# Unread matmuls placed differently around the first attention maxima of a two-layer transformer kernel

## The chip, the cores and the metric

The kernel runs on one core of one Trainium2 chip. The metric is device time in microseconds (us), the median of the runs of a kernel.

## The reference

Input x is 8 batches of 512 tokens of 128 values. Four blocks follow one another, each as x = layernorm(x + block(x)); the change touches the PE order around the first of them, causal attention with 16 heads of size 8:

```python
k, q, v = (einsum('bte,fe->btf', x, W).reshape(B, T, 16, 8) for W in (Wk, Wq, Wv))
k, q = _layernorm(k, kln_g, kln_b), _layernorm(q, qln_g, qln_b)
dot = einsum('bihd,bjhd->bhij', q * E ** -0.25, k * E ** -0.25)
att = softmax(where(causal, -inf, dot), axis=-1)
out = einsum('bte,fe->btf', einsum('bhij,bjhd->bihd', att, v).reshape(B, T, E), Wo) + bo
```

The other three are a soft mixture of 8 experts with 64 slots each, a delta-rule attention (a sequential scan) with a gated feed-forward layer, and a feed-forward layer with ternary weights.

## The kernel before

Each engine has a program of its own in which the order of its instructions is written out by hand; semaphores tie the programs together. PE, the matmul engine, runs a preparation for batch 0 and then a sequence of slots. In a slot (`slot(b, moe, front, tail, before)`) up to four batches are at work at once: `b` is in its attention scores, exponentials and products, `moe` in the experts, `tail` in the projections of the next attention, and `front` in its query, key and value projections and the first part of its row maxima. Only the first slot has a `front` and a `b` and neither of the others: `slot(0, None, 1, None, first[0])`. After the slots the second half of the kernel follows (the scan and the two feed-forward layers), from about 830 us on.

**Maxima.** The softmax needs the maximum of each row of scores. It is found with scores of its own: a batch has 24 units (`x_units`, `scores_for_maxima`). A unit is two or four matmuls of q and k on L954 (32 rows of the array each, 128 to 512 columns), two small bf16 matmuls that add the causal mask on L957, and then one DVE reduction out of PSUM on L1797. Of a batch, units x0 to x18 (`X_LATE` = 19) are run ahead, for batch 0 in the preparation and for the others at the end of a slot; the last five (e19 to e23) stand at the start of the batch's own slot, between its first scores. Units x0, x1, x12, x13 have four matmuls of 128 columns, x2, x3, x14, x15 four of 256, x4 to x7 and x16 to x18 two of 384, x8 to x11 two of 512. A unit has two PSUM banks of four, so that unit k waits until DVE has reduced unit k-2.

**Unread matmuls.** `idle_matmuls(n, bank=6)` (L964) issues n bf16 matmuls of 128x512 whose result nobody reads; they keep PE at work. In the preparation 64 of them stand between the last transposes and the maxima of batch 0, and two ahead of each unit. At the end of a slot two stand ahead of each of the units x14 to x18 (`if x_at > NM_AT`), and none ahead of x0 to x13.

**Ahead of the first unit** q and k, split in high and low parts, go to DRAM and back to be spread over the partitions. SyncE's queue writes them with six transfers (`q_rep<-hilo`, `k_rep<-hilo`, L541), each adding 16 to `split_stored`; it waits for all of them (`CREDIT + 96`) and then loads `qr` and `kr` (L546), for which unit x0 waits on PE (`rep_loaded`).

**End of the first slot.** PE runs the products of the last head group (L991), turns them (`turn_products`, L923), turns the attention (`transpose_att`, L923) and projects it (`project_att`, L1009); ACT or DVE must evacuate each before the next. Then `maxima_to` runs the units of batch 1. DVE adds the residual and works out the layer norm of batch 0 between its reductions.

Of the kernel before, what the change touches and what calls it, by code (L numbers as in the profile page):

```python
# [41 lines left out]
NM_AT, XR_AT = 13, 14  # L42
# [7 lines left out]
CREDIT = 1  # L50
# [93 lines left out]
def build(nc, A, out, taps=None):  # L144
    ctx = ExitStack()
    with ctx:
# [3 lines left out]
        def sem(name):  # L150
            return ctx.enter_context(nc.semaphore(name))
# [80 lines left out]
        class Heads:  # L232

            def __init__(self, c):
# [107 lines left out]
                  for k in range(2)]  # L342
# [35 lines left out]
        split_done, split_stored, rep_loaded = sem("split_done"), sem("split_stored"), sem("rep_loaded")  # L378
# [65 lines left out]
                  + [(A2, "n0", 4), (A2, "n1", 5), (A2, "n2", 0), (A2, "n3", 1), (A1, "fo", 3),  # L444
                     (A2, "y", 5), (A1, "x3T", 4)])
        ring2 = Ring(None, [(hand, use) for hand, use, _ in turns2], {use: bank for _, use, bank in turns2})


# [256 lines left out]
        def _(g):  # L705
# [132 lines left out]
            def out_products(t, h, half, r):  # L838

                cs = slice(half * HALF, (half + 1) * HALF)  # L840
                if r == 0:
                    g.wait_ge(hist_kept, CREDIT + t * 4 + 2 * half + 2)
                    g.wait_ge(om_summed, CREDIT + t * 8)
                    if half == 1:
                        g.wait_ge(ln3_done, CREDIT + t * DVE_LN)
                qc = s_qc[h].rearrange("p (c j) d -> p c j d", j=CH)
                _, at = PAIRS[r]
                g.tensor_tensor(o_m[half][r][:, :, :, 0:HD], state[h][:, cs, :, :],  # L848
                                qc[:, cs, r, :].unsqueeze(2).broadcast_to([P, HALF, HD, HD]), ALU.mult)
                g.tensor_tensor(o_m[half][r][:, :, :, HD:HD + r + 1], u_c[h][:, cs, :, 0:r + 1],  # L850
                                s_qkd[h][:, cs, at:at + r + 1].unsqueeze(2).broadcast_to([P, HALF, HD, r + 1]), ALU.mult) \
                    .then_inc(om_made, 1)
# [44 lines left out]
        def _(pe):  # L897
# [18 lines left out]
            def fill(use, turn):  # L916
                ring.wait_free(pe, use, *turn)
                return ps[:, ring.bank(use), :]

            def transposes(use, turn, srcs):  # L920
                bank = fill(use, turn)
                for k, src in enumerate(srcs):
                    last = pe.transpose(bank[0:src.shape[1], k * P:(k + 1) * P], src, ident[:, :])  # L923
                return last
# [15 lines left out]
            def scores_for_maxima(b, use, turn):  # L940

                k = int(use[1:])
                if k == 0:
                    pe.wait_ge(rep_loaded, CREDIT + (b + 1) * 32)
                it, pr, gs = x_units[k]
                pairs.wait_free(pe, use, *turn)
                at = pairs.bank(use)
                w = (it + 1) * P
                banks = [ps[:, at + n, 0:len(gs) * w].rearrange("p (n w) -> p n w", w=w) for n in range(2)]
                for j, gg in enumerate(gs):  # L950
                    for n, bank in enumerate(banks):
                        q = 2 * pr + n
                        rows = slice(32 * q, 32 * q + 32)
                        pe.matmul(bank[:, j, :], qr[rows, gg, it * P:(it + 1) * P], kr[rows, gg, 0:w],  # L954
                                  start=(j == 0), stop=False)
                for bank in banks:
                    last = pe.matmul(bank[:, :, it * P:w], ident_b[:, :],  # L957
                                     mask_qk[:, :].unsqueeze(1).broadcast_to([P, len(gs), P]), start=False, stop=True)
                last.then_inc(s_ready, 1)

            def idle_matmuls(n, bank=6):

                for _ in range(n):
                    pe.matmul(ps[:, bank, :], ident_b[:, :], mask_qk[:, :].unsqueeze(1).broadcast_to([P, 4, P]),  # L964
                              start=True, stop=True)

            def transpose_maxima(b, turn, h):
                pe.wait_ge(s_taken, CREDIT + b * NX + (h + 1) * (NX // 2))
                transposes(f"nm{h}", turn, [neg_max[:, 8 * h:8 * h + 8, :].rearrange("p h t -> p (h t)")]) \
                    .then_inc((f_ready, k_ready)[h], 1)  # L970
# [26 lines left out]
            def turn_products(b, turn, gg):  # L997
                pe.wait_ge(pv_act, CREDIT + V.emptied(f"pvT{gg}", b))
                transposes(f"pv{gg}", turn, [pv_T[:, gg % 2, t * P:(t + 1) * P] for t in range(NT)]).then_inc(n_ready, 1)
# [5 lines left out]
            def project_att(b, turn):  # L1005
                pe.wait_ge(n_act, CREDIT + N1.emptied("aT", b))
                bank = fill("ao", turn)
                for t in range(NT):
                    last = pe.matmul(bank[:, t * P:(t + 1) * P], act_T[:, t * P:(t + 1) * P], w_out[:, :],  # L1009
                                     start=True, stop=True)  # L1010
                last.then_inc(n_ready, 1)
# [36 lines left out]
            def expert_hidden(b, turn, c):  # L1048
                pe.wait_ge(t_act, CREDIT + T.emptied("slots", b))
                pe.matmul(fill(f"h{c}", turn), e_w1[:, c * P:(c + 1) * P], slots, start=True, stop=True) \  # L1050
                    .then_inc(t_ready, 1)
# [21 lines left out]
            def transpose_x2(b, turn):  # L1073
                pe.wait_ge(x2_ready, CREDIT + b + 1)
                transposes("x2T", turn, [y_sq[:, t, :] for t in range(NT)]).then_inc(g_ready, 1)
# [7 lines left out]
            def slot(b, moe, front, tail, before):  # L1083
# [83 lines left out]
                            products(b, gg - 1, jt)  # L1167
                if moe is not None:
                    expert_hidden(moe, turn, 0)
                if b is not None:  # L1170
                    turn_products(b, turn, 3)
                if moe is not None:
                    expert_hidden(moe, turn, 1)
                if b is not None:
# [4 lines left out]
                if tail is not None:  # L1179
                    if moe is None:  # L1180
                        idle_matmuls(40)
                    transpose_x2(tail, turn)
                if b is not None:
                    project_att(b, turn)
                x_at = 0

                def maxima_to(end):
                    nonlocal x_at
                    while x_at < end:
                        if front is not None:  # L1190
                            if x_at > NM_AT:
                                idle_matmuls(2)
                            scores_for_maxima(front, f"x{x_at}", turn)
                        x_at += 1

                maxima_to(2)
                for j in range(4):
                    if tail is not None:
                        project(tail, turn, j)
                    maxima_to(3 + j)  # L1200
                for half in range(2):
                    if moe is not None:
                        expert_out(moe, turn, (2 * half, 2 * half + 1))
                    maxima_to(8 + 2 * half)
# [26 lines left out]
            transpose_qk(0, first, 0)  # L1231
            transpose_qk(0, first, 1)
            pe.wait_ge(slot_taken, 1)
            idle_matmuls(64)
            for k in range(X_LATE):
                idle_matmuls(2)
                scores_for_maxima(0, f"x{k}", first)
                if k == NM_AT:
                    transpose_maxima(0, first, 0)
            now = slot(0, None, 1, None, first[0])  # L1240
            pe.wait_ge(w_final, 2)
            now = slot(1, 0, 2, None, now)
            now = slot(2, 1, 3, 0, now)
            with pe.Fori(0, B - 4) as i:
                slot(i + 3, i + 2, i + 4, i + 1, {N1: i + 2, K: i + 2, XE: i + 2, AS: i + 2, T: i + 1, F: i + 3, XL: i + 3, G: i})
# [952 lines left out]
```

## Time and profile before

| | us |
|---|---|
| median of 3 runs | 1388.12 |
| lowest, highest | 1379.6, 1394.48 |
| profiled execution, device time | 1389.59 |
| its span, first to last instruction | 1387.9 |
| PE busy | 1187.7 (86%) |
| DVE busy | 928.8 (67%) |
| ACT busy | 624.3 (45%) |

Times in the profile count from the first instruction. The granted clock (PEclk) is the share of PE's full clock, 2.4 GHz, that the chip let it have in a stretch: it is 1.00 or 0.50 (1.2 GHz), and a number between them is the mean of a stretch that holds both. Over the whole span it is 0.916.

### The profile page before, as it was taken

The numbers are of one execution on the slowest core, as the hardware profiler recorded it, in microseconds if no ns is written. First come the engines' busy times: TensorE is split into PE (matmuls) and PEld (weight loads), VectorE is DVE, ScalarE is ACT, GpSimd is POOL, SyncE is SP. The second block draws the span as 40 slices with busy tenths as digits, with TensorE's granted clock in tenths as the row PEclk, the third lists the DMA queues.
The fourth block names the chain that finished last, engine by engine and source line by source line (L and its number), as shares of the span: only waits on it lengthen the run. The fifth ranks groups of instructions, "written<-read, shape, count | busy, mean of one in ns | idle before, by whom it ended". The sixth has DMA issues, their size and how long they took to land.

```text
span 1387.9 us, 19758 instructions
## 1 busy us (share of the span) xinstructions
PE 1187.7 (86%) x6115; PEld 622.6 (45%) x6115; DVE 928.8 (67%) x2401; ACT 624.3 (45%) x1194; POOL 454.1 (33%) x466
## 2 busy tenths in 40 slices
PE   5898989899999899999988571158999999999997
PEld 3333445355453554535545340124455455455453
DVE  3343636556668677686865767888888888889321
ACT  1043372753736637466365320203455544645642
POOL 3022130221314333143323045125545534544510
PEclk8677899999999999999989895578999999999999
DMA  4103021032131423304212148320120220200000
GB/s 107 71 2 106 9 81 36 1 107 64 47 93 32 139 63 78 92 32 139 55 34 48 41 102 203 91 48 12 44 64 9 56 56 16 56 23 8 24 8 8
DMA packets 85755, 79.90 MB, mean 58 GB/s; under 512 B 42800, under 2 KB 63408, under 8 KB 83632
## 3 DMA queue, kind: packets, MB, share of 16 engines
q1 hardware_dynamic: 85680, 79.01, 21.0%
q8 instruction: 33, 0.54, 0.2%
q14 instruction: 42, 0.34, 0.1%
HBM read 43.17 MB, written 35.00 MB: 56 GB/s over the span
## 4 chain that ended last, share of the span: by engine, by line
PE 54%; DVE 21%; ACT 10%; issue 9%; POOL 4%; DMA 1%; SPq 1%; DVEq 0%; ACTq 0%; POOLq 0%
PE ps L1294 10%; PE ps L1277 6%; PE ps L954 5%; PE ps L923 4%; PE ps L991 4%; DVE arena L1797 4%; ACT arena L1431 3%; ACT arena L1393 3%; PE ps L957 3%; PE ps L964 3%; PE ps L980 3%; PE ps L1285 2%; PE ps L1050 2%; PE ps L1058 2%; PE ps L1040 2%
## 5 line engine op out<-in xcount | busy, mean ns | idle before, releaser
L1797 DVE TENSOR_REDUCE arena<-ps 128x4 f32<-128x512 f32 (+2 forms) x192 | 198.5, 1043 | 99.9 <-PE ps L957 96.9
L1294 PE MATMUL ps<-arena,late 128*128 128x512 f32 x512 | 224.5, 592 | 0.0
L1393 ACT ACTIVATE arena<-ps 128x512 f32<-128x512 f32 (+2 forms) x200 | 109.6, 566 | 242.8 <-PE ps L923 123.2
L753 POOL TENSOR_SCALAR_AFFINE_SELECT arena<-arena 128x512 f32<-128x512 f32 x128 | 83.5, 655 | 319.7 <-ACT arena L1431 318.4
L1431 ACT ACTIVATE arena<-ps 128x1024 f32<-128x1024 f32 (+3 forms) x256 | 169.8, 710 | 37.2 <-PE ps L980 35.8
L964 PE MATMUL ps<-mask_qk,ident_b 128*128 128x512 bf16 x447 | 129.8, 410 | 31.9 <-DVE arena L2076 31.9
L1294 PEld LDWEIGHTS ps<-arena,late 128*128 128x128 f32 x512 | 96.2, 190 | 115.8 <-issue 114.3
L1580 ACT ACTIVATE arena<-ps,f_s 128x512 f32<-128x512 f32 x128 | 85.6, 688 | 105.6 <-PE ps L1294 95.5
L1277 PE MATMUL ps<-arena,late 128*128 128x512 f32 x256 | 118.5, 617 | 7.8 <-ACT arena L1580 7.3
L923 PE MATMUL ps<-ident,arena 128*128 128x128 f32 (+1 forms) x624 | 103.8, 301 | 23.1 <-ACT arena L1393 13.5
L848 POOL TENSOR_TENSOR arena<-arena 128x512 f32<-128x512 f32 x64 | 81.5, 1273 | 119.8 <-DVE slot_T L2093 75.4
L1393 ACT ACTIVATE arena<-ps,arena 128x128 f32<-128x128 f32 (+1 forms) x128 | 62.4, 529 | 126.2 <-DVE arena L1824 52.1
L954 PE MATMUL ps<-kr,qr 32*128 32x512 f32 (+3 forms) x512 | 99.4, 427 | 15.3 <-ACT arena L1431 6.1
L991 PE MATMUL ps<-arena 128*32 128x512 f32 (+3 forms) x1024 | 99.5, 474 | 10.2 <-ACT arena L1393 10.2
L923 PEld LDWEIGHTS ps<-ident,arena 128*128 128x128 f32 (+1 forms) x624 | 74.0, 150 | 64.4 <-ACT arena L1393 23.3
L980 PE MATMUL ps<-qr,kr 32*128 32x256 f32 (+3 forms) x512 | 82.2, 435 | 18.5 <-DVE arena L1797 7.8
L954 PEld LDWEIGHTS ps<-kr,qr 32*128 32x128 f32 x512 | 47.2, 202 | 99.2 <-issue 38.2
L980 PEld LDWEIGHTS ps<-qr,kr 32*128 32x128 f32 x512 | 37.6, 193 | 110.5 <-ACT arena L1431 59.1
L1277 PEld LDWEIGHTS ps<-arena,late 128*128 128x128 f32 x256 | 49.0, 196 | 69.7 <-issue 58.3
L964 PEld LDWEIGHTS ps<-mask_qk,ident_b 128*128 128x128 bf16 x447 | 45.2, 104 | 75.9 <-issue 46.3
L1833 DVE RECIPROCAL arena<-ps 128x16 f32<-128x16 f32 x32 | 8.2, 256 | 99.3 <-PE ps L923 98.9
L957 PE MATMUL ps<-mask_qk,ident_b 128*128 128x128 bf16 (+1 forms) x384 | 66.9, 260 | 0.0
(186 smaller groups left out, 1953.4 us busy)
## 6 DMA issues: line engine op xcount, KB each, us to landing
qr<-q_rep SPq DMA_DIRECT2D x8, 1024.0 KB, 5.7
kr<-k_rep SPq DMA_DIRECT2D x8, 1024.0 KB, 8.0
scan_d<-late SPq DMA_DIRECT2D x56, 138.0 KB, 3.0
arena<-scan_d SPq DMA_DIRECT2D x12, 552.0 KB, 6.9
q_rep<-hilo SPq DMA_DIRECT2D x24, 256.0 KB, 3.1
k_rep<-hilo SPq DMA_DIRECT2D x24, 256.0 KB, 3.9
proj_d<-arena SPq DMA_DIRECT2D x8, 768.0 KB, 5.1
late<-proj_d SPq DMA_DIRECT2D x8, 768.0 KB, 4.5
```

The costliest lines, as they stand in the source:

```text
L923: last = pe.transpose(bank[0:src.shape[1], k * P:(k + 1) * P], src, ident[:, :])
L954: pe.matmul(bank[:, j, :], qr[rows, gg, it * P:(it + 1) * P], kr[rows, gg, 0:w], start=(j == 0), stop=False)
L957: last = pe.matmul(bank[:, :, it * P:w], ident_b[:, :], mask_qk[:, :].unsqueeze(1).broadcast_to([P, len(gs), P]), start=False, stop=True)
L964: pe.matmul(ps[:, bank, :], ident_b[:, :], mask_qk[:, :].unsqueeze(1).broadcast_to([P, 4, P]), start=True, stop=True)
L980: last = pe.matmul(ps[:, pairs.bank(f"s{k}") + n, 0:S - jt * P], kr[rows, gg, jt * P:(jt + 1) * P], qr[rows, gg, jt * P:S], start=True, st ...
L991: last = pe.matmul(bank[32 * h4:32 * h4 + 32, jt * P:S], v_aug[:, jt, 4 * gg + h4, :], prob[:, gg % 2, h4, p_off[jt]:p_off[jt] + S - jt * ...
L1277: return pe.matmul(ps[:, ring2.bank(use), :], w, src, start=True, stop=True)
L1294: last = pe.matmul(ps[:, ring2.bank(f"{n}{c}"), :], w[:, k, c * P:(c + 1) * P], src[:, k, :], start=(k == 0), stop=(k == HC - 1))
L1393: return act.activation(dst, src(ps[:, bank, :]), func, **kw)
L1431: act.activation(prob[:, gg % 2, 2 * pr:2 * pr + 2, p_off[jt]:p_off[jt] + w], ps[:, bank:bank + 2, 0:w], ACT.Exp).then_inc(p_taken, 1)
L1580: return act.activation(dst, src(ps[:, ring2.bank(use), :]), func, **kw)
L1797: v.tensor_reduce(heads[:, 2 * pr:2 * pr + 2, gs[0]:gs[-1] + 1], ps[:, at:at + 2, 0:len(gs) * w].rearrange("p q (n w) -> p q n w", w=w), X ...
```

## The change

Ahead of the maxima of batch 0 the 64 unread matmuls become 44, then a wait for `split_stored`, then 36; ahead of each of the 19 units one stands in place of two. In the first slot (`chain_only`), four are added ahead of `turn_products(b, turn, 3)`, four ahead of `transpose_att`, four ahead of `project_att` and two behind it, and two ahead of each of the units x0 to x13. Those in the middle of the slot write bank 0, the others bank 6. Nothing changes on the other engines.

```diff
@@ slot @@
+                chain_only = b is not None and moe is None and tail is None
+                if chain_only:
+                    idle_matmuls(4, 0)
                 if b is not None:
                     turn_products(b, turn, 3)
+                if chain_only:
+                    idle_matmuls(4, 0)
...
                     transpose_x2(tail, turn)
+                if chain_only:
+                    idle_matmuls(4, 0)
                 if b is not None:
                     project_att(b, turn)
+                if chain_only:
+                    idle_matmuls(2, 0)
...
                         if front is not None:
-                            if x_at > NM_AT:
+                            if x_at > NM_AT or chain_only:
                                 idle_matmuls(2)
                             scores_for_maxima(front, f"x{x_at}", turn)
@@ preparation @@
             pe.wait_ge(slot_taken, 1)
-            idle_matmuls(64)
+            idle_matmuls(44)
+            pe.wait_ge(split_stored, CREDIT + 96)
+            idle_matmuls(36)
             for k in range(X_LATE):
-                idle_matmuls(2)
+                idle_matmuls(1)
                 scores_for_maxima(0, f"x{k}", first)
```

PE's rows around the first unit, with the semaphores that they wait for (the first of the two unread matmuls of x0 is counted with the fill). Before:

```order
L964 MATMUL ps<-mask_qk,ident_b 128x512 [waits slot_taken]
L964 MATMUL ps<-mask_qk,ident_b 128x512 x65
L954 MATMUL ps<-kr,qr 128x128 [waits rep_loaded]
L954 MATMUL ps<-kr,qr 128x128 x3
L957 MATMUL ps<-mask_qk,ident_b 128x256 x2
L964 MATMUL ps<-mask_qk,ident_b 128x512 x2
L954 MATMUL ps<-kr,qr 128x128 x4
```

PE's rows at the same place, changed:

```order
L964 MATMUL ps<-mask_qk,ident_b 128x512 [waits slot_taken]
L964 MATMUL ps<-mask_qk,ident_b 128x512 x43
L964 MATMUL ps<-mask_qk,ident_b 128x512 [waits split_stored]
L964 MATMUL ps<-mask_qk,ident_b 128x512 x36
L954 MATMUL ps<-kr,qr 128x128 [waits rep_loaded]
L954 MATMUL ps<-kr,qr 128x128 x3
L957 MATMUL ps<-mask_qk,ident_b 128x256 x2
L964 MATMUL ps<-mask_qk,ident_b 128x512
L954 MATMUL ps<-kr,qr 128x128 x4
```

The 66 in one piece became 44 and 37 with a wait between them, and two between the units became one.

PE's rows from the last products of the first slot (L991) over the transposes (L923) and the projection (L1009) to its first units of batch 1. Before:

```order
L991 MATMUL ps<-arena 32x128 x4
L923 MATMUL ps<-ident,arena 128x128 x8
L1009 MATMUL ps<-w_out,arena 128x128 x4
L954 MATMUL ps<-kr,qr 128x128 x4
L957 MATMUL ps<-mask_qk,ident_b 128x256 x2
L954 MATMUL ps<-kr,qr 128x128 x4
L957 MATMUL ps<-mask_qk,ident_b 128x256 x2
```

PE's rows at the same place, changed:

```order
L991 MATMUL ps<-arena 32x128 x4
L964 MATMUL ps<-mask_qk,ident_b 128x512 x4
L923 MATMUL ps<-ident,arena 128x128 x4
L964 MATMUL ps<-mask_qk,ident_b 128x512 x4
L923 MATMUL ps<-ident,arena 128x128 x4
L964 MATMUL ps<-mask_qk,ident_b 128x512 x4
L1009 MATMUL ps<-w_out,arena 128x128 x4
L964 MATMUL ps<-mask_qk,ident_b 128x512 x4
L954 MATMUL ps<-kr,qr 128x128 x4
L957 MATMUL ps<-mask_qk,ident_b 128x256 x2
L964 MATMUL ps<-mask_qk,ident_b 128x512 x2
L954 MATMUL ps<-kr,qr 128x128 x4
```

Sixteen unread matmuls came in between the products and unit x0, and two ahead of each of the 13 units that follow.

## Rows read from the trace of the kernel before

**Rows 1.** Stretches of the start: each engine's busy us (x instructions), granted clock, DMA.

```profile
26.10:39.30 13.20, 13.18 (x61) 5.78 (x59) 0.00 (x0) 0.00 (x0) 4.62 (x3) 1.00 0.54 177
44.30:73.80 29.50, 29.47 (x107) 11.76 (x107) 14.98 (x16) 0.00 (x0) 0.00 (x0) 0.50 0.00 1
73.80:77.50 3.70, 3.70 (x25) 1.71 (x26) 3.27 (x4) 0.00 (x0) 0.00 (x0) 0.99 0.02 4
77.50:90.90 13.40, 11.60 (x59) 5.07 (x57) 6.84 (x7) 7.80 (x17) 4.14 (x5) 1.00 0.00 0
90.90:108.00 17.10, 15.80 (x85) 5.58 (x85) 5.91 (x14) 11.92 (x17) 5.79 (x7) 0.50 0.01 2
87.50:90.90 3.40, 2.34 (x16) 1.14 (x15) 2.35 (x2) 1.23 (x3) 2.36 (x3) 1.00 0.00 0
128.50:131.80 3.30, 2.38 (x20) 1.34 (x21) 3.14 (x13) 0.00 (x0) 1.26 (x1) 1.00 0.00 0
131.80:152.30 20.50, 19.67 (x80) 8.96 (x81) 16.50 (x31) 0.69 (x2) 0.00 (x0) 0.50 0.05 14
```

**Rows 2.** PE in order of time, fill and first unit: start, length, instructions, [idle before].

```profile
23.70 15.57 PE L964 MATMUL ps<-mask_qk,ident_b 128*128 128x512 bf16 x66
44.33 0.69 PE L954 MATMUL ps<-kr,qr 32*128 32x128 f32 x4 [5.05 <-DMA kr<-k_rep]
```

**Rows 3.** SyncE's queue in order of time: the load that follows the wait for `split_stored`.

```profile
35.61 0.37 SPq L546 DMA_DIRECT2D qr<-q_rep  x1
```

**Rows 4.** PE in order of time, the unread pairs between units at 1.2 GHz.

```profile
45.35 1.06 PE L964 MATMUL ps<-mask_qk,ident_b 128*128 128x512 bf16 x2
...
47.36 1.06 PE L964 MATMUL ps<-mask_qk,ident_b 128*128 128x512 bf16 x2
...
49.48 1.06 PE L964 MATMUL ps<-mask_qk,ident_b 128*128 128x512 bf16 x2
...
56.98 1.06 PE L964 MATMUL ps<-mask_qk,ident_b 128*128 128x512 bf16 x2
...
58.77 1.06 PE L964 MATMUL ps<-mask_qk,ident_b 128*128 128x512 bf16 x2
...
60.67 1.06 PE L964 MATMUL ps<-mask_qk,ident_b 128*128 128x512 bf16 x2
```

**Rows 5.** The same at 2.4 GHz: units with two unread matmuls, then with one.

```profile
75.44 0.59 PE L964 MATMUL ps<-mask_qk,ident_b 128*128 128x512 bf16 x2
...
76.46 0.59 PE L964 MATMUL ps<-mask_qk,ident_b 128*128 128x512 bf16 x2
...
77.93 0.38 PE L964 MATMUL ps<-mask_qk,ident_b 128*128 128x512 bf16 x1
...
78.73 0.59 PE L964 MATMUL ps<-mask_qk,ident_b 128*128 128x512 bf16 x2
```

**Rows 6.** DVE in order of time: reductions of a unit of each size.

```profile
45.60 0.69 DVE L1797 TENSOR_REDUCE arena<-ps 128x4 f32<-128x512 f32 x1 [22.71 <-PE ps L957]
...
49.72 1.23 DVE L1797 TENSOR_REDUCE arena<-ps 128x4 f32<-128x1024 f32 x1 [1.43 <-PE ps L957]
...
53.63 0.96 DVE L1797 TENSOR_REDUCE arena<-ps 128x2 f32<-128x768 f32 x1 [0.57 <-PE ps L957]
```

**Rows 7.** PE in order of time, end of the first slot.

```profile
124.59 0.66 PE L923 MATMUL ps<-ident,arena 128*128 128x128 f32 x4 [0.78 <-ACT arena L1393]
125.99 0.66 PE L923 MATMUL ps<-ident,arena 128*128 128x128 f32 x4 [0.75 <-DVE arena L1838]
127.33 1.16 PE L1009 MATMUL ps<-w_out,arena 128*128 128x128 f32 x8 [0.69 <-ACT arena L1393]
128.57 0.44 PE L954 MATMUL ps<-kr,qr 32*128 32x128 f32 x4
...
144.53 1.06 PE L964 MATMUL ps<-mask_qk,ident_b 128*128 128x512 bf16 x2
...
155.65 1.88 PE L1020 MATMUL ps<-slot_T,arena 128*128 128x512 f32 x4
```

## The prediction

> **What bounds the kernel now.** I read the granted clock first, then the stretches of the first 155 us in which it changes, and then PE, DVE and SyncE's queue in order of time inside them. The change edits nothing behind the first slot, so only this start can gain or lose by itself; the other 1230 us can differ only by where the clock falls and rises.
>
> The start is a clock story. Unread matmuls run at 2.4 GHz until about 39.3 us; then PE stands for 5.05 us until the load of kr has landed [rows 2]. When it resumes at 44.33 the clock is at 1.2 GHz, and it stays there for 29.5 us in which PE is busy without a pause, with two unread matmuls in each unit [rows 1]. There PE sets the pace: DVE needs 0.69 us for a unit of 512 scores, 0.96 for 768, 1.23 for 1024, and waits before each [rows 6]; PE's units follow each other at 2.01 us (four matmuls of 128 columns), 2.12 (four of 256), 1.79 (two of 384) and 1.90 (two of 512), read as differences between the starts of successive unread pairs [rows 4]. At 73.8 the clock returns, and a unit of two of 384 with two unread matmuls takes 1.02 us, with one 0.80 [rows 5]. The clock holds for the first third of the first slot (to 90.9), is at 1.2 GHz again to 108, and again from 131.8 to 152.3, in which the 14 units of batch 1 that have no unread matmuls lie almost whole [rows 1, 7].
>
> **The two-part fill.** An unread matmul costs 0.216 us at 2.4 GHz: 61 records in 13.2 us [rows 1]. Taking 22 away lets the first part end about 4.75 us earlier than 39.27 (15.57 us from 23.70 [rows 2]), at 34.5. PE then waits for `split_stored`. SyncE issues the load of qr right behind the same wait, at 35.61 [rows 3]; so PE stands about 1 us. 36 and the one ahead of x0 take 37 x 0.216 = 8.0 us, to about 43.6. The kr load is not touched and lands at 44.33 as before, so x0 starts at 44.33 in either kernel: the fill costs and gains nothing in itself, and no gap is over 1.1 us. Nothing but PE's own units is queued behind the new wait. The clock outlasted most of a gap of 5.05 us in the trace [rows 2], so I expect it at 2.4 GHz when x0 starts.
>
> **One unread matmul a unit.** Here I had to choose. At 2.4 GHz a 384-column unit with one is 0.80 us of PE against 0.96 of DVE, and the 512-column units are further apart (1.23 of DVE). DVE then sets the pace and PE stands for a sixth to a third of the time, its work mostly the 32-row matmuls. Which stretch is that nearest to? From 73.8 to 77.5 the units had two each, PE was busy 3.70 of 3.70 us, and the clock held. From 87.5 to 90.9 units with one each stood among first scores and waits, 2.34 of 3.40 us busy, and the clock fell at their end; from 128.5 to 131.8 units with none, 2.38 of 3.30, and it fell [rows 1]. One unread matmul in a DVE-paced row is nearer to the two that fell. So I expect the clock to hold for the first units, on the strength of the fill just before them, and to fall after about as much of such work as went before the fall at 90.9 (3.4 us), near 47.7, give or take 2. Once it is at 1.2 GHz, 29.5 us with two unread matmuls a unit did not raise it [rows 1]; one will do so less.
>
> The price: at 1.2 GHz a unit gets shorter by one unread matmul, 0.43 us (512 columns), so 1.58, 1.69, 1.36 and 1.47 us, all above DVE's time. 4 x 1.58 + 4 x 1.69 + 7 x 1.36 + 4 x 1.47 = 28.5, and 0.2 for the small transpose between: 28.7 us. The first three units at 2.4 GHz save 0.6 to 0.7 each: 26.6 us. Before, 44.33 to 77.5 were 33.2 us. **Gain 6.5 us.** (With all at 1.2 GHz, 4.5.)
>
> **What is late next.** The first slot's opening third then begins at 1.2 GHz instead of 2.4. Before, it took 13.40 us with PE busy 11.60 [rows 1]. Work of this kind stretches by 1.79 / 1.02 = 1.75 [rows 4, 5]: 11.60 x 1.75 = 20.3 us, and the small waits for ACT and DVE vanish in it. **Loss 6.9 us**, if the clock does not rise among the projections (L932) of this stretch; it can, and then half comes back. From 90.9 on the stretch was at 1.2 GHz anyway (17.1 us, busy 15.8 [rows 1]); whether a stretch of full clock comes a little earlier or later there is worth a few us either way, and I put it at zero.
>
> **The filled end of the first slot.** The four unread matmuls ahead of each of three steps take 0.86 us where PE stood 0.78, 0.75 and 0.69 [rows 7]: 0.36 us more, all told. The two behind `project_att` and the two ahead of x0 lie under DVE, whose residual and statistics begin at the end of the projection too. Sixteen unread matmuls (3.5 us at 2.4 GHz) and the transposes and projection between them (0.66 + 0.66 + 1.16) are 6 us of work with hardly a pause, so the clock should be up when x0 starts, even if it wasn't. Units x0 to x13 took 128.57 to 144.53, 16 us, although PE ran at 1.2 GHz for most of it; DVE was nearly always busy (16.50 of the 20.5 us from 131.8, nearly all in its first part) [rows 1, 7]. With two unread matmuls at 2.4 GHz PE needs 1.02 for a unit where DVE needs 0.96 and its small steps, and less than DVE elsewhere: no cost. The gain is behind them: from 144.53 to 152.3, 7.8 us at 1.2 GHz with two unread matmuls a unit, become 7.8 / 1.75 = 4.4, if the clock holds through x13: 3.4 saved. **Gain 3.0 us** with the 0.36 taken off.
>
> **The sum** is -6.5 + 6.9 - 3.0 = -2.6 us: 1387.0 by the profiled execution (1389.6), 1385.5 by the median (1388.1). The profiled execution stands 1.5 us above the median, well inside the runs' spread of 15 us, so I take the median's: 1385.5 us.
>
> **Rivals.** *One is enough*: the clock holds through all 19 units. For it: the fill now runs up to the first unit, and there is no gap over about 0.5 us. Against it: the two stretches above. Then DVE paces: four units at about 0.9, eight at 1.23 less 0.06 overlap, seven at 0.96 less 0.06, and 0.5 to the first reduction: 3.6 + 9.4 + 6.3 + 0.5 = 19.8 us, 13.4 less than before; the first third of the slot keeps its clock. 1388.1 - 13.4 - 3.0 = 1371.7. The Trainium skill (TensorE: Matmul & The Clock Gate, Part 1, "What's actually happening") says that the throttled state is the default and "activity releases the throttle", and its table "Why this matters for your kernels" asks only that there be no long idle gaps between bursts. By it this rival would be the outcome. The trace disagrees in part: 29.47 of 29.50 us busy at a clock of 0.50 [rows 1].
>
> *Rise among the projections*: as forecast, but the clock comes back within the slot's first third. Half of 6.9: 1382.
>
> *Slower, the clock falls in the second row of units*: those of 512 columns last 1.23 us on DVE with 2 x 0.216 unread in them, a thinner mix than the 384-column units for which the trace shows a held clock. If it falls at x8, PE needs 1.90, 2.01 instead of 1.23 and 0.8 to 1.2 for six units: about 0.67 x 4 + 0.9 x 2 = 4.5 us lost, and the 3.4 behind them are not gained. Sum -6.5 + 6.9 + 0.4 + 4.5 = +5.3: 1393. It decides from the first unit at 1.2 GHz; if that were x0, all 14 would run as at 45 to 70 us, 27 us instead of 16, and the time would be 1400.
>
> *The fill doesn't do what it says*: if the clock were at 1.2 GHz when the second part starts, 37 x 0.43 = 15.8 us would end at 51.4, 7 us behind kr's landing. Then 28.7 us of units: +7.1 - 4.5 + 6.9 - 3.0 = +6.5, 1395. The gap before it is only 1 us, so this is unlikely.
>
> **Chances.** Forecast 0.47, rise among the projections 0.18, one is enough 0.2, slower by the second row 0.1, slower by the fill 0.05. A median of this kernel can tell about 1% (14 us) from no change, seen from its spread. Faster by over 1% (under 1374.2) is the rival of 1371.7, nearly whole, and a little of the others by luck of the clock: 0.2. Slower by over 1% (over 1402) needs the extreme of the slower rivals: 0.03. Within: 0.77. The range must hold 8 in 10: from 1371, which takes in most of the fast rival, to 1394, which takes in the slower one and the spread of the median.
>
> **What would show it.** In the changed profile: unread matmuls in two pieces with about 1 us between, the second ending near 43.6; x0 at 44.3. The clock at 1.00 then and falling between 46 and 50. Units of two of 384 follow at 1.36 us. (If instead at 0.90, with DVE idle nowhere, one was enough.) The first slot's first scores near 71, at 1.2 GHz. At its end, gaps ahead of L923 and L1009 gone and the clock at 1.00 from there to the second slot; the stretch from x14 to L1020, 11.1 us before [rows 7], near 8. What would make me wrong: the clock held by one unread matmul, or the first slot's middle, whose 24 us at 1.2 GHz I left as they are.

## The result and the profile after

| | before | changed |
|---|---|---|
| median, us | 1382.64 (20 runs) | 1374.99 (20 runs) |
| lowest to highest | 1373.6 to 1397.04 | 1365.78 to 1382.6 |
| profiled execution, device time | 1389.59 | 1370.53 |
| mean granted clock of it | 0.916 | 0.939 |

The ratio is 0.994, with a 95% interval of 0.9912 to 0.9967: 7.7 us or 0.6% faster in the median. Ratios leave out executions more than 1.5% above the fastest of their kernel, so one can lie nearer to 1 than the medians beside it. The two profiled executions differ by 19.1 us, more than twice what the medians differ by: the one before lies 7 us above its median, the one after 4.5 us below its own.

The stretches of the start, as in [rows 1] (engines' busy time, granted clock, DMA):

```profile
28.10:44.70 16.60, 15.88 (x73) 6.88 (x71) 0.00 (x0) 0.00 (x0) 3.20 (x3) 1.00 0.71 237
44.70:63.50 18.80, 17.22 (x112) 8.02 (x113) 17.02 (x19) 0.00 (x0) 0.00 (x0) 1.00 0.01 2
63.50:75.80 12.30, 10.48 (x52) 4.61 (x50) 6.04 (x7) 7.42 (x16) 3.75 (x4) 1.00 0.01 1
75.90:82.60 6.70, 6.10 (x28) 1.86 (x30) 5.51 (x12) 2.86 (x4) 1.41 (x2) 0.50 0.00 0
...
103.20:136.10 32.90, 32.05 (x227) 15.75 (x224) 23.28 (x50) 3.36 (x8) 3.69 (x4) 1.00 0.22 73
```

The second line is the answer to the 29.50 us at 0.50 of [rows 1]: all 19 units ran at 2.4 GHz with one unread matmul each, and DVE was busy 17.02 of 18.80 us. DVE in order of time:

```profile
47.40 10.98 DVE L1808 TENSOR_REDUCE arena<-ps 128x4 f32<-128x1024 f32 x11 [0.28 <-PE ps L957]
```

Eleven reductions follow one another without a pause, so from x2 on DVE sets the pace. The clock then held for 12.3 us of the first slot.

PE in order of time, for [rows 2], [rows 4] and [rows 5], and SyncE's row for [rows 3]:

```profile
24.28 11.54 PE L964 MATMUL ps<-mask_qk,ident_b 128*128 128x512 bf16 x44
36.22 8.16 PE L964 MATMUL ps<-mask_qk,ident_b 128*128 128x512 bf16 x37 [0.40 <-DMA k_rep<-hilo]
44.72 0.44 PE L954 MATMUL ps<-kr,qr 32*128 32x128 f32 x4 [0.34 <-DMA kr<-k_rep]
...
50.31 0.38 PE L964 MATMUL ps<-mask_qk,ident_b 128*128 128x512 bf16 x1
...
51.18 0.38 PE L964 MATMUL ps<-mask_qk,ident_b 128*128 128x512 bf16 x1
...
53.82 0.38 PE L964 MATMUL ps<-mask_qk,ident_b 128*128 128x512 bf16 x1
54.44 0.50 PE L954 MATMUL ps<-kr,qr 32*128 32x512 f32 x2 [0.24 <-DVE arena L1808]
...
55.00 0.38 PE L964 MATMUL ps<-mask_qk,ident_b 128*128 128x512 bf16 x1
```

```profile
36.19 0.37 SPq L546 DMA_DIRECT2D qr<-q_rep  x1
```

The pause at the new wait was 0.40 us, the one ahead of x0 0.34. Two units of 384 columns follow each other at 0.87 us (50.31 to 51.18), two of 512 at 1.18 (53.82 to 55.00); in the second pair PE waits 0.24 us for DVE, in the first it doesn't.

PE at the end of the first slot, for [rows 7]:

```profile
108.83 0.63 PE L923 MATMUL ps<-ident,arena 128*128 128x128 f32 x4
...
110.20 0.66 PE L923 MATMUL ps<-ident,arena 128*128 128x128 f32 x4
...
111.56 1.15 PE L1009 MATMUL ps<-w_out,arena 128*128 128x128 f32 x8
...
113.50 0.44 PE L954 MATMUL ps<-kr,qr 32*128 32x128 f32 x4
...
128.56 0.59 PE L964 MATMUL ps<-mask_qk,ident_b 128*128 128x512 bf16 x2
...
136.16 1.88 PE L1020 MATMUL ps<-slot_T,arena 128*128 128x512 f32 x4
```

The idle time ahead of the three steps is gone, and they follow each other as before: 1.37 and 1.36 us, against 1.40 and 1.34. From turn_products(3) to L1020 it is 27.3 us, where it was 31.1. Most of that lies behind x13: from the unread matmuls of x14 to L1020 it took 7.6 us (128.56 to 136.16) where it had taken 11.1. Units x0 to x13 gained 0.9 us, and the way from L1009 to x0 got 0.7 longer, 1.94 us for 1.24, with the added unread matmuls in it.

The 19.1 us between the two profiled executions add up as follows: the start 0.4 later, x0 to the first slot 33.1 to 18.8 (-14.4), the slot's opening and middle 47.1 to 45.3 (-1.8), its end -3.7, all the rest of the kernel 1232.2 to 1232.6.

### The profile page after: what moved, and what is told of

Read it like the earlier page. It is cut to its first block, busy times and chain, and to the rows that moved or that the text cites. A ratio compares the mean times of both kernels' runs of the same rounds, so it can differ in the third digit from the quotient of the medians.

```text
span 1368.8 us, 19836 instructions
## 1 busy us (share of the span) xinstructions
PE 1171.7 (86%) x6154; PEld 617.6 (45%) x6154; DVE 925.4 (68%) x2401; ACT 623.5 (46%) x1194; POOL 453.4 (33%) x466
## 4 chain that ended last, share of the span: by engine, by line
PE 49%; DVE 25%; ACT 10%; issue 9%; POOL 5%; DMA 1%; SPq 0%; ACTq 0%; DVEq 0%; POOLq 0%
PE ps L1305 9%; PE ps L1288 5%; DVE arena L1808 5%; PE ps L954 4%; PE ps L923 4%; PE ps L991 4%; ACT arena L1442 4%; ACT arena L1404 3%; PE ps L957 3%; PE ps L980 3%; PE ps L964 2%; PE ps L1050 2%; PE ps L1058 2%; PE ps L1296 2%; DVE arena L2075 2%
## 5 line engine op out<-in xcount | busy, mean ns | idle before, releaser
L1442 ACT ACTIVATE arena<-ps 128x1024 f32<-128x1024 f32 (+3 forms) x256 | 169.8, 710 | 36.9 <-PE ps L980 35.7
L964 PE MATMUL ps<-mask_qk,ident_b 128*128 128x512 bf16 x486 | 133.1, 390 | 32.5 <-DVE arena L2087 32.1
L923 PE MATMUL ps<-ident,arena 128*128 128x128 f32 (+1 forms) x624 | 102.3, 298 | 25.1 <-ACT arena L1404 12.8
L991 PE MATMUL ps<-arena 128*32 128x512 f32 (+3 forms) x1024 | 97.8, 467 | 11.1 <-ACT arena L1404 11.1
L923 PEld LDWEIGHTS ps<-ident,arena 128*128 128x128 f32 (+1 forms) x624 | 73.2, 149 | 65.7 <-ACT arena L1404 22.5
L954 PE MATMUL ps<-kr,qr 32*128 32x512 f32 (+3 forms) x512 | 91.3, 393 | 11.2 <-ACT arena L1442 6.1
L964 PEld LDWEIGHTS ps<-mask_qk,ident_b 128*128 128x128 bf16 x486 | 47.1, 100 | 79.1 <-issue 47.3
L954 PEld LDWEIGHTS ps<-kr,qr 32*128 32x128 f32 x512 | 42.9, 183 | 88.1 <-issue 29.1
L1296 PEld LDWEIGHTS ps<-late,arena 128*128 128x128 f32 x512 | 60.3, 192 | 11.7 <-issue 7.2
```

The costliest lines, as they stand in the source:

```text
L991: last = pe.matmul(bank[32 * h4:32 * h4 + 32, jt * P:S], v_aug[:, jt, 4 * gg + h4, :], prob[:, gg % 2, h4, p_off[jt]:p_off[jt] + S - jt * ...
L1296: last = pe.matmul(ps[:, ring2.bank(use), j * P:(j + 1) * P], hid[:, c, j * P:(j + 1) * P], w[:, c, :], start=(c == 0), stop=(c == HC - 1))
L1442: act.activation(prob[:, gg % 2, 2 * pr:2 * pr + 2, p_off[jt]:p_off[jt] + w], ps[:, bank:bank + 2, 0:w], ACT.Exp).then_inc(p_taken, 1)
```

## The experiments

For every profiled execution the table gives three stretches of PE's program, each with the part of it that was at 1.2 GHz in brackets: from x0 to the first slot's first transposes, from there to turn_products(3), and from there to L1020; then all that follows to the end.

| kernel | x0 to slot | slot to turn_products(3) | to L1020 | rest |
|---|---|---|---|---|
| before | 33.1 (29.5) | 47.1 (23.9) | 31.1 (20.5) | 1232.2 |
| before again | 35.7 (35.5) | 54.8 (43.0) | 30.2 (17.1) | 1234.4 |
| changed | 18.8 (0) | 45.3 (13.7) | 27.3 (0) | 1232.6 |
| changed again | 18.8 (0) | 44.5 (10.2) | 27.3 (0) | 1237.8 |
| changed, third | 21.9 (9.4) | 49.6 (24.8) | 27.3 (0) | 1234.3 |
| preparation alone | 24.1 (17.0) | 45.4 (13.7) | 31.2 (23.9) | 1227.2 |
| slot's fills alone | 21.8 (3.4) | 44.4 (10.2) | 27.3 (0) | 1230.7 |
| two a unit | 20.3 (0) | 47.1 (23.9) | 27.3 (0) | 1232.6 |
| two a unit, again | 20.3 (0) | 43.8 (10.2) | 27.3 (0) | 1230.3 |
| none a unit | 20.9 (18.1) | 50.8 (36.5) | 27.3 (0) | 1234.7 |
| one piece of 65 | 28.2 (28.2) | 53.2 (43.4) | 27.3 (0) | 1229.5 |
| one piece of 85 | 21.8 (9.1) | 50.0 (31.9) | 27.3 (0) | 1230.4 |
| two on x4 to x11 | 19.2 (0) | 44.5 (10.2) | 27.3 (0) | 1234.1 |
| three ahead of e19 to e23 | 20.3 (0) | 51.0 (23.9) | 27.3 (0) | 1231.1 |

The last column has no edit in it and still runs from 1227.2 to 1237.8 us, a spread larger than most of the effects looked for. So what an edit does is read from the first three columns, and whether it pays from medians.

**The preparation alone.** The first slot is that of the kernel before.

```diff
-            idle_matmuls(64)
+            idle_matmuls(44)
+            pe.wait_ge(split_stored, CREDIT + 96)
+            idle_matmuls(36)
             for k in range(X_LATE):
-                idle_matmuls(2)
+                idle_matmuls(1)
```

> The kernel before with the change of the preparation alone (44, wait, 36, one unread matmul a unit); the first slot has no added unread matmuls. Clock theory (the gain of the preparation is that the clock does not fall while kr is awaited): x0 at about 44.7 at a granted clock of 1.00, the first slot's transposes (L923) near 63.5, and the first slot's end, from turn_products(3) to L1020, as before, 31 us; so 3 to 4 us behind the changed kernel, some 4 to 5 us ahead of the one before in the median. Rival, the first slot's fills carry most of the gain: the median is that of the kernel before within 2 us, although the profile shows the preparation shorter.

Median 1376.78 (12 runs) beside 1382.96 for the kernel before (35 runs); ratio 0.9966, interval 0.993 to 1.0002. The stretches of its profile:

```profile
44.70:51.70 7.00, 6.61 (x45) 3.21 (x45) 5.77 (x7) 0.00 (x0) 0.00 (x0) 1.00 0.00 0
51.80:68.70 16.90, 16.90 (x68) 7.01 (x67) 12.27 (x13) 0.00 (x0) 0.00 (x0) 0.50 0.00 1
```

Up to x18 this program is the changed one. Here the clock did fall among the units, 7 us after x0, with one pause of PE before it, of 0.25 us; so one unread matmul a unit doesn't always hold it. The end of the slot took 31.2 us, as expected. The interval, which takes in no change, leaves both theories standing on their size.

**The first slot's fills alone.** The preparation is that of the kernel before (64, two a unit).

```diff
-            idle_matmuls(44)
-            pe.wait_ge(split_stored, CREDIT + 96)
-            idle_matmuls(36)
+            idle_matmuls(64)
             for k in range(X_LATE):
-                idle_matmuls(1)
+                idle_matmuls(2)
```

> The kernel before with the first slot's added unread matmuls alone; preparation as before (64, two a unit). Clock theory: the preparation is as before (clock 0.50 from the end of the gap until about 74), the stretch from turn_products(3) to L1020 goes from 31 us to 27.3; the median is 3 to 4 us below that of the kernel before. Rival (the fills only fill gaps that cost nothing): within 1 us of it, either way.

Median 1377.51 (12 runs), ratio 0.996 (0.9916 to 1.0005). The end of the slot fell to 27.3 us, the 3.8 us expected. What I had not expected stands in the preparation:

```profile
44.50:47.80 3.30, 3.30 (x16) 1.43 (x14) 1.15 (x2) 0.00 (x0) 0.00 (x0) 0.50 0.00 0
47.90:66.00 18.10, 18.10 (x113) 8.07 (x113) 16.32 (x18) 0.00 (x0) 0.00 (x0) 1.00 0.01 2
```

The instructions are those of the kernel before and PE stood 4.20 us ahead of x0 where it had stood 5.05, and the clock came back after 3.4 us instead of 30.7. The shorter gap doesn't explain it: with 4.29 us the kernel before stayed down for 61.4 us (below). The stretch took 21.8 us, not 33. The interval takes in no change, so the times alone don't show that the slot's fills pay; the profiles do.

**Two unread matmuls a unit.** The changed kernel with `idle_matmuls(35)` in the second part and `idle_matmuls(2)` ahead of each unit.

```diff
-            idle_matmuls(36)
+            idle_matmuls(35)
             for k in range(X_LATE):
-                idle_matmuls(1)
+                idle_matmuls(2)
```

> The changed kernel with two unread matmuls ahead of each unit of the first maxima in place of one (35 in the second fill). Clock theory: the clock holds through the units, a 384-column unit takes 1.02 us instead of 0.96, the 19 units about 20 us instead of 18.8, so 1 us slower than the changed kernel in an execution where both hold; where one unread matmul is too little to hold the clock in some executions, two are ahead in the median by up to 5 us. Count theory (what is gained are 19 x 0.43 us of unread matmuls at 1.2 GHz): 8 us slower than the changed kernel.

Median 1372.43 (12 runs), ratio 0.9918 (0.9884 to 0.9953), the lowest median of the four kernels timed on this chip.

```profile
45.60:65.80 20.20, 20.20 (x129) 9.26 (x130) 17.60 (x19) 0.00 (x0) 0.00 (x0) 1.00 0.01 2
65.90:79.20 13.30, 11.50 (x59) 4.97 (x57) 6.79 (x7) 7.80 (x17) 4.09 (x5) 1.00 0.00 0
```

20.2 us at 2.4 GHz, PE without a pause: 1.5 us more than with one, and not 8. The count theory falls: the gain isn't the unread matmuls taken out, but the clock at which everything else runs.

Beside the kernel with the slot's fills alone this is also the plainest test of the fill, since the two differ in nothing else: 66 unread matmuls in one piece there, 44, the wait and 37 here, two a unit and the slot's fills in both. The medians are 1377.51 and 1372.43, 5.1 us apart, and the slowest of 12 executions were 1395.85 and 1377.07.

**No unread matmul a unit.** 37 in the second part, none ahead of the units.

```diff
-            idle_matmuls(36)
+            idle_matmuls(37)
             for k in range(X_LATE):
-                idle_matmuls(1)
                 scores_for_maxima(0, f"x{k}", first)
```

> The changed kernel with no unread matmul ahead of the units of the first maxima (37 in the second fill). If a DVE-paced row of units without them does not hold the clock, as in 128.5 to 131.8 of the kernel before: it falls within some 5 us of x0, the units take about 21 us (1.15, 1.26, 0.96 and 1.23 us each, nearly DVE's own pace) and the first slot's first third 20 instead of 13.4 us; 8 us slower than the changed kernel. If PE's clock needs no help there: 0 to 1 us faster than the changed kernel.

Median 1377.14 (12 runs), ratio 0.9955 (0.9922 to 0.9988).

```profile
45.80:48.50 2.70, 2.60 (x22) 1.49 (x23) 1.71 (x3) 0.00 (x0) 0.00 (x0) 1.00 0.00 1
48.60:66.60 18.00, 16.68 (x71) 7.24 (x71) 15.97 (x17) 0.00 (x0) 0.00 (x0) 0.50 0.01 1
66.70:103.10 36.40, 34.07 (x142) 12.96 (x140) 12.83 (x21) 19.97 (x34) 9.79 (x11) 0.50 0.01 2
```

The clock fell 2.8 us behind x0, as expected of a row without them, and stayed down for 54.6 us. The units cost only 20.9 us, for without unread matmuls they are short at 1.2 GHz too, DVE busy for 15.97 of 18.00 us; the loss is in the first slot, 50.8 us in place of 45.3. The size expected, 8 us, was that of the profile (7.5 from x0 to L1020, of it 5.5 in the slot); the median of 12 lies 2 us behind the changed kernel's 1374.99, and 4.7 behind that of two a unit on the same chip.

**The gap put back.** The changed kernel with the fill in one piece of 65 and one unread matmul a unit.

```diff
-            idle_matmuls(44)
-            pe.wait_ge(split_stored, CREDIT + 96)
-            idle_matmuls(36)
+            idle_matmuls(65)
```

> The changed kernel with the fill in one piece again (65 unread matmuls, no wait for split_stored, so PE stands some 5 us before x0) and one unread matmul a unit. If the second part of the fill is what keeps the clock: it falls at the end of the gap and, with one unread matmul a unit, stays at 1.2 GHz through the units (28 us for x0 to x18 against 18.8) and mostly through the first slot's opening third; 10 to 15 us slower than the changed kernel, that is slower than the kernel before. If the second part matters little because the clock comes back soon after the gap: within 3 us of the changed kernel.

Median 1383.79 (12 runs), ratio 1.0017 (0.9984 to 1.005).

```profile
44.30:72.50 28.20, 28.17 (x111) 12.02 (x112) 18.52 (x19) 0.00 (x0) 0.00 (x0) 0.50 0.00 1
72.60:109.00 36.40, 34.08 (x142) 12.93 (x140) 12.63 (x20) 19.97 (x34) 9.82 (x11) 0.50 0.01 2
```

Without the second part no gain is left in the times, although the slot's end still took 27.3 us. That is 8.8 us behind the changed kernel's 1374.99 (the two were not timed side by side), a little less than the 10 to 15 I expected, and it isn't clearly slower than the kernel before. This execution is what I forecast for the changed kernel: 28.2 us of units, all at 1.2 GHz (I had 28.7), and an opening of the slot at 1.2 GHz (53.2 us to turn_products(3) against 47.1 before, 6.1 more; I had 6.9).

**The kernel before, again.** No edit.

> The kernel before once more, one look, to see where its clock falls and comes back in another execution. If the 30 us at 1.2 GHz behind the gap are the rule: x0 to the first slot again 33 us. If that profile was an unlucky execution: the clock comes back within some us of x0, as in the kernel with the first slot's fills alone, and the stretch takes about 22 us.

1401.39 us, one execution.

```profile
44.60:80.30 35.70, 35.70 (x130) 14.14 (x131) 18.52 (x19) 0.00 (x0) 0.00 (x0) 0.50 0.00 1
80.30:106.10 25.80, 24.14 (x86) 8.73 (x84) 12.08 (x18) 11.62 (x21) 5.22 (x7) 0.50 0.00 0
```

With the same preparation the clock has now been seen to be away for 3.4, 30.7 and 61.4 us behind the gap. The 30 us of [rows 1] were neither the rule nor bad luck, but one of several outcomes.

**The changed kernel, again.** No edit.

> The changed kernel once more, one look. If one unread matmul a unit always holds the clock: 18.8 us from x0 to the first slot again. If it holds only in some executions, as in the kernel with the preparation alone where it fell at 51.8: a fall among the units, and 21 to 26 us.

1374.78 us, one execution; the clock held through the units again.

```profile
44.60:63.40 18.80, 17.20 (x111) 8.01 (x112) 17.01 (x19) 0.00 (x0) 0.00 (x0) 1.00 0.01 2
```

**Three unread matmuls ahead of e19 to e23**, in the kernel with two a unit, in the first slot alone (part of the edit shown).

```diff
-                        idle_matmuls(1)
+                        idle_matmuls(3 if chain_only else 1)
```

> The kernel with two unread matmuls a unit in the first maxima, and three in place of one ahead of the units e19 to e23 in the first slot, where the clock fell in every profile at about 15 us into that slot. If that fall comes from the thin mix there: it comes later or not at all, and saves up to 3 us against two a unit alone; if it comes from the waits for DVE behind them, which the added work only fills: no change, or 1 to 2 us slower by the ten matmuls added.

Median 1374.6 (12 runs) beside 1385.62 for the kernel before (23 runs); ratio 0.9956 (0.9927 to 0.9984).

```profile
65.10:80.20 15.10, 13.30 (x65) 5.62 (x62) 6.77 (x7) 7.81 (x17) 4.20 (x5) 1.00 0.00 0
80.30:87.10 6.80, 6.20 (x33) 1.61 (x31) 5.36 (x12) 3.56 (x4) 0.98 (x3) 0.50 0.00 0
```

The ten matmuls made the opening longer (15.1 us up to the fall, 13.3 with one each) and the clock fell at about the same place in the program, at e23. No gain.

**One piece of 85, no wait.**

```diff
-            idle_matmuls(44)
-            pe.wait_ge(split_stored, CREDIT + 96)
-            idle_matmuls(36)
+            idle_matmuls(85)
```

> The changed kernel with one fill of 85 unread matmuls and no wait for split_stored (5 more than 44 + 36, for the time that PE stood at the wait). It fills the same time without a pause of 0.4 to 1 us. If all that matters is that PE is at work until kr lands: within 1 us of the changed kernel, x0 at the same time. If the pause at the wait costs the clock in some executions: faster in the median by up to 3 us. If 85 overshoot kr's landing: x0 later by the overshoot, under 1 us.

Median 1373.92 (12 runs), ratio 0.9951 (0.9913 to 0.9989). PE in order of time:

```profile
23.71 20.00 PE L964 MATMUL ps<-mask_qk,ident_b 128*128 128x512 bf16 x86
44.24 0.44 PE L954 MATMUL ps<-kr,qr 32*128 32x128 f32 x4 [0.53 <-DMA kr<-k_rep]
```

The same time as the split fill, whose median was 1373.97 on the same chip. The wait for `split_stored` isn't what helps; that PE is at work until kr lands is.

**Two, one, and a mix, side by side.** Two a unit once more, the changed kernel once more, and

```diff
-                idle_matmuls(1)
+                idle_matmuls(2 if 4 <= k < 12 else 1)
```

> Two unread matmuls a unit once more, now beside the changed kernel on the same chip. If one unread matmul loses the clock in part of the executions (as in the kernel with the preparation alone) and two never do: 1.4 us longer from x0 to the first slot (20.3 against 18.8), but 2 to 3 us less than the changed kernel in the median and fewer executions over 1376. If one always holds it: 1 to 2 us more than the changed kernel.

> The changed kernel, timed beside the three others. Median 1375, two groups of executions, near 1371 and near 1378; the upper group has the lower mean clock (0.93 against 0.94), which is the fall among the units and in the first slot's opening third.

> The changed kernel with two unread matmuls ahead of x4 to x11 (the units of 384 and 512 columns, where the row of one each is thinnest) and one ahead of the others. If the clock is lost only in that stretch: as good as two everywhere or up to 1 us better, about 19.5 us from x0 to the first slot. If it is also lost in the others: between one and two in the median.

Medians of 12 on one chip, the kernel before at 1387.14 (35 runs): two 1373.49 (ratio 0.9938, 0.99 to 0.9976), one 1373.97 (0.9972, 0.9929 to 1.0014), mix 1374.07 (0.9959, 0.992 to 0.9998). The 2 to 3 us by which I expected two to be ahead of one didn't show. The twelve executions of the changed kernel do leave a gap, seven up to 1374.25 and five from 1378.88, with mean clocks of 0.932 to 0.941 and 0.923 to 0.933. The third profile of the changed kernel shows what the first two did not:

```profile
44.30:56.80 12.50, 11.48 (x74) 5.30 (x75) 11.22 (x12) 0.00 (x0) 0.00 (x0) 1.00 0.00 0
56.80:66.20 9.40, 9.40 (x40) 4.08 (x39) 6.38 (x8) 0.00 (x0) 0.00 (x0) 0.50 0.01 3
66.20:77.30 11.10, 11.10 (x33) 4.46 (x31) 3.15 (x3) 5.31 (x10) 0.72 (x2) 0.50 0.00 0
77.30:84.10 6.80, 5.15 (x27) 2.27 (x26) 4.25 (x4) 2.98 (x9) 3.67 (x4) 1.00 0.01 2
```

The clock fell at 56.8, at the end of the 512-column units, and came back among the slot's projections, at 77.3. The kernel with one piece of 85 lost it at 57.0 and had it back at 74.1. In both, no pause of PE between the fill and the fall was over 0.53 us. In all three profiles with two a unit, the one with three ahead of e19 to e23 among them, it held to the end of the row, and in the mix too. So two look the safer choice by these few traces, at 1.5 us in the row, and the times can't tell them apart: two a unit had medians of 1372.43 and 1373.49, one a unit 1374.99 and 1373.97.

## Why the prediction was right or wrong

The time was in the range and on the forecast side: 1375.0 against 1385.5 with 1371 to 1394. But the net of 2.6 us was too small beside 7.7, and that the time still fell in the range is in part luck: the sum started from a base 5.5 us too high, and the range was wide enough to hold the rival whose mechanism ran in two of the three profiles of the changed kernel.

- **The two-part fill**: right. x0 came at 44.72, 44.64 and 44.29 against 44.33, the second part ran at 2.4 GHz for 8.16 us (8.0 worked out), and its pauses were 0.40, 1.10 and 1.70 us at the wait (about 1 worked out), 0.34 to 0.50 ahead of x0. In two of the variants the load of kr landed some 1.2 us later, x0 came at 45.54 and 45.76 behind a pause of 1.42 and 1.32 us, and the clock was up all the same. For the clock in the gap before, the prediction points at [rows 2], which don't show it; this stretch of the kernel before does:

```profile
39.30:44.30 5.00, 0.00 (x0) 0.00 (x0) 0.00 (x0) 0.00 (x0) 0.00 (x0) 0.88 0.88 321
```

A mean of 0.88 in 5.00 us is 1.2 us at 0.50 at its end, so it had outlasted most of the gap, as said.

- **One unread matmul a unit: the clock falls near 47.7.** This step failed. I took a row of units with one each for nearest to the two stretches of [rows 1] in which it fell. It held for all 18.8 us in two profiles of the changed kernel, for 12.5 us in the third, for 12.7 in the one with a piece of 85 and for 7 us in the one with the preparation alone. Only the row with none lost it as soon as I forecast, after 2.8 us. The rival "one is enough" had it right in kind (13.4 us less expected, 14.4 measured) for the first two, and my forecast in kind for the other three, but 4 to 9 us later than I put it. That the same kernel can go either way from one execution to the next was missing from the cases altogether.
- **Units at 1.2 GHz**: right in size, 28.2 us measured with the gap put back for 28.7.
- **The slot's opening third at 1.2 GHz, 6.9 us lost**: right in size (6.1 there, 7.7 in the second profile of the kernel before, against the first), but the changed kernel paid it in none of its three profiles in full. In two the clock held for 12.4 and 13.1 us of the slot; in the third it came back at 77.3, which is the rival "rise among the projections".
- **Before, a clock that stays away**: I took 33.2 us for what the kernel before costs. In three profiles of its preparation it cost 21.8, 33.1 and 35.7, and 19.1 us of difference between two profiles became 7.7 between medians. The 1388.1 of three runs that I took the sums from was high too, by 5.5 us against the median of 20. So the fast rival, right about the mechanism in two of three profiles, had 16.4 us where the medians have 7.7, and landed near the time (1371.7 for 1375.0) only because its base was high.
- **The slot's filled end, 3.0 gained**: 3.4 less 0.36 expected, 27.3 us in every profile of a kernel that has it, with the clock at 1.00 from end to end, against 31.1, 30.2 and 31.2 in the three without: 2.9 to 3.9. From x14 on it was 3.5 us for 3.4; the unread matmuls between `project_att` and x0, which I had put under DVE at no cost, cost 0.7, and units x0 to x13, put at nothing, gave 0.9. The 0.36 for over-full gaps was not paid. The slower rival, a fall among x8 to x11, came in none of them.
- **The middle at zero**: 47.1 and 54.8 before, 44.5, 45.3 and 49.6 changed. But two profiles of the one kernel with two a unit had 47.1 and 43.8, so the few us aren't shown to be the change's doing.

What stays open is why the clock comes back at one time after 3.4 us and at another after 61 with the same instructions, and how often each happens; the runs give profiles of three executions of the one preparation and four of the other, too few for shares. The rule of the Trainium skill that I set against the forecast ("activity releases the throttle", TensorE: Matmul & The Clock Gate, Part 1) fits the executions in which the clock held. It doesn't fit the falls at 51.7, 56.8 and 57.0, with no pause of PE over 0.53 us between the fill and them, nor the second profile of the kernel before, where PE was busy 35.70 of 35.70 us at a clock of 0.50.

## What to carry to other kernels

Where a matmul engine must wait for a transfer ahead of a long row of small, 32-row matmuls, fill the whole wait up to the first of them. With the gap put back the row took 28.2 us against 18.8 to 21.9 and the stage behind it 53.2 against 44.5 to 49.6; in the medians the fill was worth 5.1 us with two unread matmuls a unit, timed side by side, and 8.8 with one, not side by side. One and two could not be told apart by time. Read two or three profiles before sizing a clock effect; the same preparation gave anything from 21.8 to 35.7 us here. And don't judge how long a mix of work holds the clock from a stretch that has longer waits in it beside the thin work: taken from one, my fall came 4 to 9 us too early, and in two executions there was none.

## What the runs showed of the hardware

- The same row of some 130 instructions, PE never idle, ran at 1.2 GHz for 35.7 us in one execution, and in another for 3.3 us and then at 2.4 GHz.
- A clock lost at the gap reaches far: with the gap put back it stayed at 1.2 GHz for 64.9 us, through the whole opening of the first slot.
- The units without unread matmuls took 20.9 us with the clock at 1.2 GHz for 18.1 of them, those with two each 20.3 and those with one each 18.8, all at 2.4 GHz: where they held the clock, one or two unread matmuls a unit made the row no longer than none did. The next stage took 50.8 us behind the first, 47.1 and 43.8 behind the second.
- A full clock lasted through a pause of 3.8 us ahead of x0 and fell in the rest of it, in the kernel before; with pauses of 1.3 to 1.7 us in the filled wait it was at 1.00 in every profile.
